# Alternating the closing steps of one attention half with the opening steps of the next, and running the down products one chunk later in place of two, in a four-layer cross-attention and feed-forward kernel

## The chip, the cores and the metric

The kernel is one program on one core of a Trainium2 chip. The metric is device time in microseconds (us) of one execution: 1136.41 us, the median of 3 runs. About 0.5% of it (5.7 us) is what a comparison can tell from no change.

## The reference

The input x has 4 batch rows ("streams") of 512 tokens by 128 features; the context has 77 tokens for each stream. Four layers follow one another, each an attention half and a feed-forward half, both added to x through a gate:

```
for l in 0..3:
    x = x + tanh(g_xattn[l]) * attention_l(layernorm(x), ctx)
    x = x + tanh(g_ffn[l])   * feed_forward_l(layernorm(x))
```

- attention 0, 1, 2: 16 heads of width 8, softmax over the 77 keys; attention 1 first works out a temperature for each head from statistics of the softmax; attention 2 has a padding mask. Attention 3 is one wide head with ReLU projections.
- feed-forward 0: 64 inner units with 16 hidden each; 1: a mixture of 4 experts of width 512, SiLU gated, top 2; 2: RMS norm and 8 experts of width 352, SiLU gated, top 2; 3: 8 linear experts, top 2.

All is float32; the expert products are made of three products of rounded parts.

## The kernel before, in words

The weights are loaded and turned once (the first 65 us). After that everything is in SBUF, and the only later transfers are the four stores of the result.

A *half* is one attention or one feed-forward of one layer and stream. Halves named ("A", i) for i = 0 to 11 are the multi-head attentions (kind A0 for i = 0 to 3, A1 for 4 to 7, A2 for 8 to 11); ("A", 12) to ("A", 19) are attention 3 and feed-forward 3 of the streams in turn (kinds A3, F3). ("F", 0) to ("F", 11) are the feed-forwards of layers 0 to 2 (kinds F0, F1, F2). So there are two tracks. Half ("F", i) runs beside ("A", i + 2), `beside` at line 727; ("F", 10) has 12 to 15 beside it and ("F", 11) has 16 and 17. I call such a pair of halves a stage.

Each engine (TensorE for matmuls, VectorE, ScalarE, GpSimd) has a queue of its own and works it off in order, with semaphores between engines. The order is fixed by hand: every half is a generator of *steps* on each engine, and all engines walk the same list `ORDER`. `turns` (line 729) makes it: `merged` (line 100) interleaves the steps of the attention half and of the feed-forward half of a stage in proportion to weights (`weights_a`, `weights_f`), so that both come to their ends together. A step's weight is thus the share of the other track that is laid beside it, not a time. A step that waits holds up all that stands behind it on its engine.

A multi-head half has three parts:

- `pre`, 28 steps (38 for A1). Step 0: VectorE takes the LayerNorm statistics (line 1034), GpSimd makes the inverse deviation (lines 804, 806); in kind A0 TensorE transposes the context (1372), which ScalarE copies in step 1. Step 2: K and V products on TensorE (1378, 1383), normalising on VectorE (1047), which waits for GpSimd. Step 3: ScalarE copies K and V out (868, 872), TensorE transposes the normalised x into bank `c` (1359). Step 4: ScalarE copies it to `xfa` (854), VectorE adds the rounding rest of K (1114). Step 5: VectorE lays the keys out by head (1128), and TensorE makes the first of four Q products (1392). Steps 9 to 24 (`S0` to `S1`) are 16 score blocks for the row maxima (1404, 1142), in A1 with exponentials and sums too.
- `body`, 17 steps: scores, exponential, product with V, and the turning of each group of four heads.
- `tail`, 7 steps, a chain across engines: ScalarE copies the last group out (`copy_out`, 846), TensorE turns it (`turn`, 1345), VectorE divides it (`divide`, 1018, 1020), TensorE transposes the whole (1665), ScalarE copies that (999), TensorE makes the product with Wo (1672, 1674), and VectorE adds it to x (1317).

`attention` (line 764) runs `pre`, `body` and `tail` of each half, and then those of the next. I call the steps from the last copy-out (846) of one half to the first Q product (1392) of the next a *seam*; there are eleven between the twelve multi-head halves.

The feed-forwards F1 and F2 go through 16 and 24 *chunks*, three steps each. TensorE makes the up product into a bank `UP` (three matmuls, lines 1585 to 1587), ScalarE takes a tanh of it into `hb` (983), VectorE multiplies (1286); TensorE makes the gate product into bank 5, VectorE multiplies by it (1277, signal `chunk_ready`). The gate product of the next chunk needs bank 5, and so waits for that signal. The `down` product (1597) takes `hb` and adds into bank 7; it is called `LATE` = 2 chunks later, and when an expert is whole VectorE adds it to x (`gated`, 1266). `hb` has three buffers: the tanh of chunk n waits for the down product of chunk n - 3.

Of the kernel before, what the change touches and what calls it, by code (L numbers as in the profile page):

```python
# [34 lines left out]
ACT = mybir.ActivationFunctionType  # L35
AX = mybir.AxisListType

P = 128
# [5 lines left out]
S2 = 77  # L44
S2E = S2 + S2 % 2
H = 16
HD = 8
G = 4
# [8 lines left out]
ATTENTIONS = 3 * STREAMS  # L57
# [5 lines left out]
F2 = 352  # L63
# [487 lines left out]
def main(nc, a, out, v):  # L551

    ctx, sb, sig, bank = v["ctx"], v["sb"], v["sig"], v["bank"]
# [3 lines left out]
    WqR, WkR, Wv, Wo, bo, ones_r, bcol, W3x, diag = (v[n] for n in (  # L557
        "WqR", "WkR", "Wv", "Wo", "bo", "ones_r", "bcol", "W3x", "diag"))
# [5 lines left out]
    KT, VP, lg, pk = (v[n] for n in ("KT", "VP", "lg", "pk"))  # L564

    m1_w1, m1_w3, m1_w2, m2_w1, m2_w2, m2_w3, m2_rms, m3_w, m3_b = (v[n] for n in (
        "m1_w1", "m1_w3", "m1_w2", "m2_w1", "m2_w2", "m2_w3", "m2_rms", "m3_w", "m3_b"))
# [12 lines left out]
    x, ctxn, mk, mr, x2p = (v[n] for n in ("x", "ctxn", "mk", "mr", "x2p"))  # L580
    in_x, in_ctx, masks_ready = (v[n] for n in ("in_x", "in_ctx", "masks_ready"))
    ctxT = each("ctxT", [P, S2])


    xfa = sb("xfa", [P, N])
    xff = two("xff", [P, N]) + [xfa]
    xna, xnf = sb("xna", [P, T, P]), sb("xnf", [P, T, P])
# [79 lines left out]
    NS = T * G  # L667
# [6 lines left out]
    S0 = Q0 + G  # L674
    S1 = S0 + NS
    RING = (1, 0, 2, 3)
    TURN = (4, 5)
    LATE = 2

    def ends_expert(k, n):  # L680
        return n + 1 == len(chunks[k]) or chunks[k][n + 1][0] > chunks[k][n][0]
# [13 lines left out]
    def steps_pre(k):  # L695
        if k in MHA:
            return S1 + (13 if k == "A1" else 3)
        return {"F0": 5, "A3": 12}.get(k, 11)

    def steps_body(k):  # L700
        if k in MHA:
            return H + 1
        return {"A3": 3, "F0": 2 * (C0 + 1), "F3": len(tiles)}.get(k) or 3 * (len(chunks[k]) + LATE)

    def steps_tail(k):
        return 7 if k in MHA else 2 if k == "F0" else 0

    def weights_a(u):

        k = kind(u)  # L710
        if k in MHA:
            block, after = (1.8, 0.8) if k == "A1" else (0.5, 0.6)
            return [1.0] * S0 + [block] * NS + [after] * (steps_pre(k) - S1) + [0.75] * steps_body(k) + [0.6] * steps_tail(k)
        return [1.0] * (steps_pre(k) + steps_body(k))

    def steps_f(u):
# [43 lines left out]
    UP = ups()  # L760

    def run(pre, body, tail):

        def attention():
            for i in range(ATTENTIONS + 2 * STREAMS):
                u = ("A", i)
                yield from chain(pre(u), body(u), tail(u))

        def feed_forward():
            yield from pre(("F", 0))  # L770
            for i in range(ATTENTIONS):
                u, n = ("F", i), steps_f(("F", i))
                last = i + 1 == ATTENTIONS
                m, ahead = (0, iter(())) if last else (steps_pre(kind(("F", i + 1))), pre(("F", i + 1)))
                sent = 0
                for at, _ in enumerate(chain(body(u), tail(u))):
                    while sent < m and (sent + 1) * n <= (at + 1) * m:
                        next(ahead)
                        sent += 1
                    yield  # L780
                assert sent == m and at + 1 == n and next(ahead, None) is None

        tracks = {"A": attention(), "F": feed_forward()}
        for half in ORDER:
            next(tracks[half])
        assert all(next(t, None) is None for t in tracks.values())

    with nc.Block() as block:
# [49 lines left out]
        def _(act):  # L838
# [9 lines left out]
            def pre(u):  # L848
                half, s, k, b = u[0], side(u), kind(u), stream(u)
                l = int(k[1])  # L850

                def normalized():
                    act.wait_ge(*x_turned.at(u, T - 1))
                    act.activation((xfa if half == "A" else xff[s])[:], bank[2 if half == "A" else UP[u, "x"]][:], ACT.Copy, scale=m2_rms[:, 0:1] if k == "F2" else 1.0) \  # L854
                        .then_inc(*xf_ready.up(u))

                for i in range(steps_pre(k)):
                    if k in MHA:
# [3 lines left out]
                        if i == 3:  # L862

                            if u[1]:
                                act.wait_ge(*keys_ready.at(("A", u[1] - 1), J - 1))
                            act.wait_ge(*k_psum.at(u))
                            for g in range(G):
                                act.activation(Ksp[:, g, :].bitcast(F32R), bank[0][0:QK, g * S2:(g + 1) * S2], ACT.Identity,
                                               bias=bcol[0:QK, l, 1, g:g + 1],
                                               accum_out=ksum[0:QK, g:g + 1] if l == 1 else None).then_inc(*k_high.up(u, g))  # L870
                            act.wait_ge(*v_psum.at(u))
                            act.activation(VP[:, :, 0:HD],
                                           bank[1][0:S2, 0:P].rearrange("p (h d) -> p h d", d=HD), ACT.Copy,
                                           scale=mk[b][:, 1:2] if l == 2 else 1.0).then_inc(*values_ready.up(u))
                        if i == 4:
                            normalized()
                        if Q0 < i <= Q0 + G:
# [449 lines left out]
        def _(pe):  # L1327
            reader = {}

            def free(b):  # L1330
                if b in reader:
                    signal, *key = reader[b]
                    pe.wait_ge(*signal.at(*key))
# [15 lines left out]
            def pre(u):  # L1349
                half, s, k, y = u[0], side(u), kind(u), stream(u)  # L1350
                l = int(k[1])

                c, xn, xf = (2, xna, xfa) if half == "A" else (UP[u, "x"], xnf, xff[s])

                def transpose_x():
                    free(c)
# [6 lines left out]
                for i in range(steps_pre(k)):  # L1363
# [4 lines left out]
                    if k in MHA:  # L1368
# [5 lines left out]
                        if i == 2:  # L1374
                            free(0)
                            pe.wait_ge(*ctx_ready.at(y))
                            for g in range(G):
                                op = pe.matmul(bank[0][0:QK, g * S2:(g + 1) * S2], WkR[l][:, g, :], ctxT[y][:], start=True, stop=True)
                            op.then_inc(*k_psum.up(u))
                            reader[0] = (k_low, u, G - 1)  # L1380

                            free(1)
                            pe.matmul(bank[1][0:S2, 0:P], ctxT[y][:], Wv[l][:], start=True, stop=True).then_inc(*v_psum.up(u))
                            reader[1] = (values_ready, u)
                        if i == 3:
                            transpose_x()
                        if Q0 <= i < S0:
                            g = i - Q0
                            b = RING[g % 4]
                            pe.wait_ge(*xf_ready.at(u))  # L1390
                            free(b)
                            pe.matmul(bank[b][0:QK, :], WqR[l][:, g, :], xf[:], start=True, stop=True).then_inc(*q_psum.up(u, g))  # L1392
                            reader[b] = (q_low, u, g)
                        if S0 <= i < S1:
                            n = i - S0
                            t, g = n // G, n % G
                            b = RING[(G + n) % 4]
# [75 lines left out]
                    elif k in router:  # L1473
                        w, b, E = router[k]
# [243 lines left out]
```

## Time and profile before

| what | us |
|---|---|
| median of 3 runs (1135.51 to 1141.63) | 1136.41 |
| the profiled execution, its own time | 1137.24 |
| its span, first to last instruction | 1135.5 |
| TensorE busy | 944.7 |
| VectorE busy | 711.9 |
| ScalarE busy | 459.6 |
| mean granted TensorE clock | 0.912 of full |

Busy time is the time in which an engine works on an instruction; a wait on a semaphore is not busy. A wait is put down to the instruction that ended it. In the profile, PE is TensorE, PEld its weight loads, DVE VectorE, ACT ScalarE and POOL GpSimd; L1317 is line 1317 of the kernel. A float32 product is two or more matmul instructions, so a line's count is larger than the number of products.

### The profile page before, as it was taken

The page shows a single profiled execution, that of the slowest core. Times are in us where ns is not written, and L with a number is a line of the kernel's source. Part 1 is how long each engine was busy: PE and PEld are TensorE (multiplying, and loading weights), DVE is VectorE, ACT ScalarE, POOL GpSimd, SP SyncE. Part 2 cuts the span into 40 slices and gives each one's busy share as a digit, 9 for nine tenths or more (in the row PEclk, how much of TensorE's full clock was granted, in tenths as well). Part 3 has the DMA queues.
Part 4 walks back from the last instruction along what each step waited for, and adds up shares of the span by engine and source line. Part 5 has one row for each costly group of instructions (what it writes and reads, how often), then busy time and mean ns, then how long its engine had stood idle before and what let it go on. Part 6 is the DMA issues. An engine that isn't in the chain of part 4 may idle for free.

```text
span 1135.5 us, 14471 instructions
## 1 busy us (share of the span) xinstructions
PE 944.7 (83%) x4795; PEld 624.7 (55%) x4795; DVE 711.9 (63%) x2190; ACT 459.6 (40%) x1101; POOL 105.9 (9%) x175
## 2 busy tenths in 40 slices
PE   2468899887777886987899899999999888979967
PEld 1434444433333355656567667666767666657744
DVE  0871433517538369579585665776776578887845
ACT  1515345455647645645635316335325222212110
POOL 3100000002103013012000100100100100000000
PEclk8669789999678898998999989999999899999987
DMA  9300000000000000000000000000000000000000
GB/s 262 118 1 1 1 1 1 1 1 1 0 1 1 1 1 1 1 1 1 1 1 2 1 1 1 1 1 1 1 1 1 1 1 10 1 10 1 1 10 9
DMA packets 12065, 12.72 MB, mean 11 GB/s; under 512 B 3758, under 2 KB 7896, under 8 KB 11992
## 3 DMA queue, kind: packets, MB, share of 16 engines
q10 hardware_dynamic: 5536, 8.04, 2.4%
q1 hardware_dynamic: 6072, 3.24, 1.1%
q0 software_dynamic: 384, 0.53, 0.3%
q8 instruction: 39, 0.64, 0.2%
q14 instruction: 34, 0.28, 0.1%
HBM read 10.75 MB, written 1.05 MB: 10 GB/s over the span
## 4 chain that ended last, share of the span: by engine, by line
PE 53%; DVE 28%; ACT 6%; issue 5%; POOL 2%; POOLq 0%; ACTq 0%; DVEq 0%
PE bank L1597 9%; PE bank L1585 5%; PE bank L1507 5%; PE bank L1587 4%; PE bank L1586 4%; PE bank L1392 4%; PE bank L1522 4%; DVE x L1302 3%; DVE hb L1286 3%; DVE nm L1142 3%; DVE hb L1277 3%; DVE x L1266 2%; PE bank L1562 2%; ACT PTs L946 2%; PE bank L1568 2%
## 5 line engine op out<-in xcount | busy, mean ns | idle before, releaser
L983 ACT ACTIVATE hb<-bank 96x512 f32<-96x512 f32 (+1 forms) x160 | 95.5, 597 | 262.6 <-PE bank L1587 261.7
L1585 PE MATMUL bank<-parts,m_w_lo 128*96 128x512 f32 (+1 forms) x320 | 151.0, 472 | 37.0 <-DVE hb L1277 30.0
L1597 PEld LDWEIGHTS bank<-m_w,hb 128*128 128x128 f32 (+1 forms) x1280 | 166.2, 197 | 26.8 <-issue 11.9
L1597 PE MATMUL bank<-m_w,hb 128*128 128x128 f32 (+1 forms) x1280 | 178.8, 284 | 0.5
L1286 DVE SCALAR_TENSOR_TENSOR hb<-hb,bank 96x512 f32<-96x512 f32 (+1 forms) x160 | 108.9, 680 | 87.8 <-ACT hb L983 87.4
L1587 PE MATMUL bank<-parts,m_w_hi 128*96 128x512 f32 (+1 forms) x320 | 128.9, 403 | 0.0
L1586 PE MATMUL bank<-parts,m_w_hi 128*96 128x512 f32 (+1 forms) x320 | 128.7, 402 | 0.0
L1277 DVE TENSOR_TENSOR hb<-hb,bank 96x512 f32<-96x512 f32 (+1 forms) x160 | 109.8, 686 | 11.5 <-PE bank L1587 6.4
L1585 PEld LDWEIGHTS bank<-parts,m_w_lo 128*96 128x96 f32 (+1 forms) x320 | 60.3, 189 | 82.6 <-DVE hb L1277 47.2
L1522 PE MATMUL bank<-Qs,KT 112*77 112x512 f32 x192 | 96.6, 520 | 6.8 <-ACT PTs L946 5.6
L1018 DVE RECIPROCAL rden<-bank 128x16 f32<-128x16 f32 x48 | 12.2, 255 | 130.8 <-PE bank L1345 130.8
L1142 DVE TENSOR_REDUCE nm<-bank 128x4 f32<-128x308 f32 x192 | 84.0, 471 | 15.6 <-PE bank L1412 10.4
L1404 PE MATMUL bank<-KT,Qs 96*128 96x308 f32 x192 | 77.0, 426 | 17.2 <-ACT PTs L892 12.5
L804 POOL TENSOR_SCALAR rstd_a<-mv_a 128x4 f32<-128x4 f32 x20 | 4.6, 228 | 830.5 <-DVE mv_a L1037 830.5
L1266 DVE SCALAR_TENSOR_TENSOR x<-bank,gw,x 128x128 f32<-128x128 f32 x192 | 53.9, 343 | 26.4 <-PE bank L1597 25.7
L1587 PEld LDWEIGHTS bank<-parts,m_w_hi 128*96 128x96 f32 (+1 forms) x320 | 59.9, 187 | 16.3
L1586 PEld LDWEIGHTS bank<-parts,m_w_hi 128*96 128x96 f32 (+1 forms) x320 | 60.4, 189 | 9.2 <-issue 3.4
L1404 PEld LDWEIGHTS bank<-KT,Qs 96*128 96x128 f32 x192 | 38.1, 202 | 42.2 <-ACT PTs L892 22.9
L1392 PE MATMUL bank<-xfa,WqR 128*96 128x512 f32 x96 | 54.2, 681 | 2.7 <-ACT xfa L854 2.7
L892 ACT ACTIVATE PTs<-bank,nms 128x77 f32<-128x77 f32 x128 | 39.9, 328 | 37.0 <-DVE nms L1161 37.0
L1507 PE MATMUL bank<-PTs,VP 77*32 77x512 f32 x384 | 54.5, 614 | 0.0
L846 ACT ACTIVATE Os<-bank 128x512 f32<-128x512 f32 x48 | 28.7, 598 | 61.0 <-PE bank L1507 61.0
(272 smaller groups left out, 1544.0 us busy)
## 6 DMA issues: line engine op xcount, KB each, us to landing
m_w<-in_L_ffn_w_dram ACTq DMA_DIRECT2D x2, 1024.0 KB, 11.4
nat_m<-in_L_ffn_W_dram ACTq DMA_DIRECT2D x1, 1408.0 KB, 16.7
x<-in_x_dram SPq DMA_DIRECT2D x4, 256.0 KB, 8.1
out_dram<-x SPq DMA_DIRECT2D x4, 256.0 KB, 2.0
f_out<-in_L_ffn_Wout_dram POOLq DMA_DIRECT2D x8, 64.0 KB, 7.9
m_w<-in_L_ffn_W_experts_dram ACTq DMA_DIRECT2D x1, 512.0 KB, 17.1
ctxn<-in_ctx_dram SPq DMA_DIRECT2D x4, 38.5 KB
Wq<-in_L_xattn_Wq_dram SPq DMA_DIRECT2D x2, 64.0 KB
```

The costliest lines, as they stand in the source:

```text
L983: act.activation(hb[n % 3][0:m, :], bank[UP[u, n]][0:m, :], ACT.Tanh, scale=0.5).then_inc(*chunk_act.up(u, n))
L1142: dve.tensor_reduce(nm[:, t, J * g:J * g + J], bank[RING[(G + n) % 4]][:, 0:J * S2].rearrange("p (h k) -> p h k", k=S2), AX.X, ALU.max, ne ...
L1277: dve.tensor_tensor(h, h, bank[TURN[1]][0:m, :], ALU.mult).then_inc(*chunk_ready.up(u, n))
L1286: dve.scalar_tensor_tensor(out=h, in0=h, scalar=1.0, in1=bank[UP[u, n]][0:m, :], op0=ALU.add, op1=ALU.mult) \
L1392: pe.matmul(bank[b][0:QK, :], WqR[l][:, g, :], xf[:], start=True, stop=True).then_inc(*q_psum.up(u, g))
L1404: op = pe.matmul(dst, Qs[0:QK, g, t * P:(t + 1) * P], KT[0:QK, J * g:J * g + J, :].rearrange("p h k -> p (h k)"), start=True, stop=l == 1)
L1507: op = pe.matmul(bank[2 + g % 2][32 * j:32 * j + 32, :], VP[:, h, :], PT[h % NPT][0:S2, :], start=True, stop=True, tile_position=(0, 32 * j))
L1522: pe.matmul(dst, KT[:, h, :], Qs[0:QK + H, h // J, :], start=l != 0, stop=True).then_inc(*scores_psum.up(u, h))
L1585: pe.matmul(dst, w_lo, x_hi, start=True, stop=False)
L1586: pe.matmul(dst, w_hi, x_hi, start=False, stop=False)
L1587: return pe.matmul(dst, w_hi, x_lo, start=False, stop=True)
L1597: op = pe.matmul(bank[7][:, t * P:(t + 1) * P], hb[n % 3][0:m, t * P:(t + 1) * P], wd, start=i == 0 and t == 0, stop=ends_expert(k, n) and ...
```

## The change

Three things are edited, and what they need.

1. In `attention`, the first `EARLY` = 6 steps of the next half's `pre` are issued between the seven steps of the tail, in turn: tail 0, pre 0, tail 1, pre 1, to tail 5, pre 5, tail 6. This is for the eleven seams between the halves 0 to 11; the tail of half 11, and everything after it, keep their order. The thirteen steps have a weight of 0.5 each; they had 0.6 for a step of the tail and 1.0 for each of the six. The six belong to the list of the earlier half now, so that they lie beside another feed-forward half than before.
2. So that both can be under way, banks are moved: the normalised x is turned into bank 1 (2 for A3 and F3), and V comes to stand beside K in bank 0, and is made and copied before K. The Q product into bank 0 waits for that copy as well.
3. `LATE` is 1 in place of 2: the down product of chunk n - 1 follows the gate product of chunk n, and a half of kind F1 or F2 has three steps fewer at its end.

```
-    LATE = 2
+    EARLY = 6
+    XA = {"A3": 2, "F3": 2}
+    LATE = 1
...
-            return [1.0] * S0 + [block] * NS + [after] * (steps_pre(k) - S1) + [0.75] * steps_body(k) + [0.6] * steps_tail(k)
+            pre = [1.0] * S0 + [block] * NS + [after] * (steps_pre(k) - S1)
+            tail = [0.6] * steps_tail(k) if u[1] + 1 == ATTENTIONS else [0.5] * (steps_tail(k) + EARLY)
+            return pre[EARLY if u[1] else 0:] + [0.75] * steps_body(k) + tail
...
         def attention():
+            ahead = pre(("A", 0))
             for i in range(ATTENTIONS + 2 * STREAMS):
-                u = ("A", i)
-                yield from chain(pre(u), body(u), tail(u))
+                yield from chain(ahead, body(("A", i)))
+                ahead = pre(("A", i + 1))
+                for at, _ in enumerate(tail(("A", i))):
+                    yield
+                    if i + 1 < ATTENTIONS and at < EARLY:
+                        next(ahead)
+                        yield
...
-                    act.activation((xfa if half == "A" else xff[s])[:], bank[2 if half == "A" else UP[u, "x"]][:], ACT.Copy, scale=m2_rms[:, 0:1] if k == "F2" else 1.0) \
+                    act.activation((xfa if half == "A" else xff[s])[:], bank[XA.get(k, 1) if half == "A" else UP[u, "x"]][:], ACT.Copy, scale=m2_rms[:, 0:1] if k == "F2" else 1.0) \
...
                             act.wait_ge(*k_psum.at(u))
+                            act.wait_ge(*v_psum.at(u))
+                            act.activation(VP[:, :, 0:HD],
+                                           bank[0][0:S2, G * S2:G * S2 + P].rearrange("p (h d) -> p h d", d=HD), ACT.Copy,
+                                           scale=mk[b][:, 1:2] if l == 2 else 1.0).then_inc(*values_ready.up(u))
...
-                            act.wait_ge(*v_psum.at(u))
-                            act.activation(VP[:, :, 0:HD],
-                                           bank[1][0:S2, 0:P].rearrange("p (h d) -> p h d", d=HD), ACT.Copy,
-                                           scale=mk[b][:, 1:2] if l == 2 else 1.0).then_inc(*values_ready.up(u))
...
-                c, xn, xf = (2, xna, xfa) if half == "A" else (UP[u, "x"], xnf, xff[s])
+                c, xn, xf = (XA.get(k, 1), xna, xfa) if half == "A" else (UP[u, "x"], xnf, xff[s])
...
                             pe.wait_ge(*ctx_ready.at(y))
+                            pe.matmul(bank[0][0:S2, G * S2:G * S2 + P], ctxT[y][:], Wv[l][:], start=True, stop=True) \
+                                .then_inc(*v_psum.up(u))
...
-                            free(1)
-                            pe.matmul(bank[1][0:S2, 0:P], ctxT[y][:], Wv[l][:], start=True, stop=True).then_inc(*v_psum.up(u))
-                            reader[1] = (values_ready, u)
...
                             free(b)
+                            if b == 0:
+                                pe.wait_ge(*values_ready.at(u))
```

## Rows read from the trace of the kernel before

**Rows 1.** The page: busy time by engine, and granted clock in 40 slices.
```profile
PE 944.7 (83%) x4795; PEld 624.7 (55%) x4795; DVE 711.9 (63%) x2190; ACT 459.6 (40%) x1101; POOL 105.9 (9%) x175
...
PEclk8669789999678898998999989999999899999987
```
**Rows 2.** Windows by stage: stretch, length, busy (count) of each engine, PEclk, DMA.
```profile
67.00:111.92 44.92, 38.51 (x189) 19.76 (x188) 15.56 (x43) 18.43 (x36) 1.28 (x2) 0.88 0.00 1
...
259.69:334.15 74.46, 54.63 (x174) 24.75 (x173) 37.17 (x115) 43.31 (x130) 13.50 (x20) 0.76 0.00 1
...
571.25:641.24 69.99, 67.78 (x388) 48.08 (x386) 47.29 (x134) 29.96 (x55) 2.52 (x4) 1.00 0.00 1
...
892.34:1135.50 243.16, 200.31 (x1085) 151.46 (x1083) 176.37 (x566) 46.57 (x86) 13.01 (x22) 0.93 0.01 5
```
**Rows 3.** Windows of the eleven seams: the first, the sum of the first six, the sum of all.
```profile
105.61:116.78 11.17, 6.48 (x33) 4.76 (x33) 5.67 (x29) 3.15 (x9) 2.51 (x4) 0.70 0.00 0
...
sum 70.97, PE 46.92 PEld 32.92 DVE 32.04 ACT 25.93 POOL 8.80; mean PE 7.82 PEld 5.49 DVE 5.34 ACT 4.32 POOL 1.47
...
sum 149.07, PE 111.55 PEld 84.92 DVE 84.23 ACT 52.35 POOL 21.74; mean PE 10.14 PEld 7.72 DVE 7.66 ACT 4.76 POOL 1.98
```
**Rows 4.** PE's waits from 105.6 to 892 us: total, times, longest.
```profile
PE bank L1585 <- DVE hb L1277: 18.7, 21, 2.1
...
PE bank L1665 <- DVE att L1020: 9.7, 12, 1.4
...
PE bank L1359 <- DVE xna L1047: 8.6, 7, 2.1
...
PE bank L1345 <- ACT Os L846: 4.7, 6, 0.8
PE bank L1672 <- ACT Os L999: 3.8, 6, 0.8
```
**Rows 5.** Timeline of the third seam, on PE.
```profile
208.49 1.16 PE L1674 MATMUL bank<-Wo,Os 128*128 128x128 f32 x8
...
213.45 1.01 PE L1359 MATMUL bank<-ident,xna 128*128 128x128 f32 x4 [1.95 <-DVE xna L1047]
...
215.16 1.09 PE L1392 MATMUL bank<-xfa,WqR 128*96 128x512 f32 x2
```
**Rows 6.** Timeline of the third seam, on DVE and ACT.
```profile
210.35 0.86 DVE L1034 BATCH_NORM_STATS2 stats_a<-x 128x6 f32<-128x128 f32 x4
...
212.96 1.11 DVE L1047 TENSOR_SCALAR xna<-x,mv_a,rstd_a 128x128 f32<-128x128 f32 x4 [1.46 <-POOL rstd_a L806]
214.11 0.92 DVE L1114 SCALAR_TENSOR_TENSOR Ksp<-bank,bcol,Ksp 32x77 f32<-32x77 f32 x4
...
215.14 1.24 DVE L1128 TENSOR_SCALAR KT<-Ksp,hmask 96x308 fp32r<-96x308 f32 x4
...
204.56 0.60 ACT L846 ACTIVATE Os<-bank 128x512 f32<-128x512 f32 x1 [1.73 <-PE bank L1507]
...
211.38 0.96 ACT L868 ACTIVATE Ksp<-bank,bcol 96x77 fp32r<-96x77 f32 x4
212.23 0.28 ACT L872 ACTIVATE VP<-bank 77x128 f32<-77x128 f32 x1
```
**Rows 7.** PE in the stretches of half clock that begin in seams or just behind.
```profile
110.10:120.40 10.30, 7.89 (x26) 0.50 0.00 0
...
sum 30.70, PE 26.59; mean PE 5.32
```
**Rows 8.** Timeline of the tenth seam, where the eighth feed-forward half begins.
```profile
719.16 0.50 PE L1585 MATMUL bank<-parts,m_w_lo 128*128 128x512 f32 x1 [2.13 <-DVE hb L1277]
...
716.02 0.74 DVE L1317 SCALAR_TENSOR_TENSOR x<-bank,gates_col,x 128x512 f32<-128x512 f32 x1
716.68 0.86 DVE L1034 BATCH_NORM_STATS2 stats_a<-x 128x6 f32<-128x128 f32 x4
...
718.42 0.69 DVE L1277 TENSOR_TENSOR hb<-hb,bank 128x512 f32<-128x512 f32 x1
```

## The prediction, made before the changed kernel was run

> **What bounds the kernel now.** I read the busy times of the page first, then the windows stage by stage, then the waits of PE, and last the timeline of single seams.
>
> PE is busy for 944.7 of 1135.5 us, DVE for 711.9, ACT for 459.6 [rows 1]. The reader is to see that no engine is full over the whole, but PE comes near, and that its clock is below full in the first half of the span and nearly full later. By stage there are three pictures [rows 2]. In the first ones (attention 0, alone or beside the light feed-forward 0) PE idles 44.92 - 38.51 = 6.4 us of 44.9. Where attention 1 lies beside feed-forward 0 nothing is full: PE 54.6, ACT 43.3 and DVE 37.2 of 74.5 us, at a mean clock of 0.76; here a chain across engines sets the time. With the expert halves PE is full: 67.8 of 70.0 us at full clock. In the last 243 us PE idles 43 us, but that stretch keeps its order, but for `LATE`.
>
> So where the first edit works, time is to be had only from PE's idle time and from its clock. The windows of the eleven seams give 149.07 us with PE busy for 111.55: 37.5 us idle, a quarter of the seams' length, against 2 us idle in a whole 70 us stage elsewhere [rows 2, 3]. PE's waits say what for [rows 4]: for the divided heads 9.7 us, the normalised x 8.6, the copy-outs 4.7 and 3.8. These are the links of two chains, the tail and the opening, run one after the other. (A few of the copy-out waits lie in a body, outside a seam.)
>
> **The change part by part.** *The alternation.* I take the third seam. It lasts from 204.56, where the copy-out starts, to the first Q product at 215.16: 10.6 us [rows 5, 6]. The tail's chain takes half of that, and the statistics of the next stream, which need nothing from it, start only at 210.35 [rows 6]. Now I lay the same instructions out in the new order, from the copy-out at 0, each in order on its engine. ACT: copy-out to 0.6. PE: turning the group 0.75 to 1.4. DVE: statistics 0 to 1.2, dividing from 1.4 to 1.95 (0.55 for its two instructions). POOL is done at 2.6, since 212.96 - 210.35 = 2.6 us pass from the start of the statistics to normalising, at which DVE now starts. PE: K and V from 1.4 to 2.6 (eight and two small matmul instructions; I allow 1.2 us), the divided heads to 3.2, x turned from 3.0 to 3.95. ACT: V and K together 1.24 us [rows 6], to 3.9, then the tail's copy to 4.5, and x to 5.1. PE: the product with Wo from 4.6 to 5.7 (1.16 us for its matmuls, [rows 5]), and the first Q product at 5.7. DVE: the rest of K and the keys (0.92 and 1.24 us, [rows 6]) end near 6.2, and the addition to x near 7.0.
>
> So a bare seam is 5.7 us long, of which PE works about 5, in place of 10.6. The feed-forward's share comes on top. By the weights of attention 0 the seam had (4.2 + 6) of 35.75, or 28.5% of the feed-forward beside it, and has 6.5 of 32.05, or 20%. That work goes nowhere else for free: it fills the blocks and the body, where PE is full in most stages. I count no gain for the move of it, only for the idle time. PE's waits by name in the seams and around them add up to 9.7 + 8.6 + 4.7 + 3.8 = 26.8 us [rows 4]. I take it that two thirds of them go, 18 us. The ends: nothing, if the alternated chains wait as long as the two did, and all 37.5 us of the seams [rows 3]. I choose near the middle, since my layout leaves some 0.7 us in a bare seam, and eleven of that are 8 us.
>
> *The clock.* Granted clock falls to half (1.2 of 2.4 GHz) just behind five of the seams. In the first seam PE was busy for 6.48 of 11.17 us, and from 110.1 the clock was half for 10.3 us, with PE busy for 7.89 of them. The five stretches make 30.7 us with PE busy for 26.59 [rows 3, 7]. At full clock their matmuls would need about half: 13.3 us is the upper end, and the lower is nothing, if the clock falls there all the same, or somewhere else. PE in the seams will be busy for some 80% in place of 75% on average, and in the first from 58% to near 85%. I take 6 us, a little under half of the upper end, because part of what a matmul takes in those stretches is already hidden behind ACT and DVE.
>
> [...] In this trace no single gap in the seams is longer than 2.1 us [rows 4], and the clock fell all the same. [...]
>
> *Work ahead of the chunks.* Where an expert half begins, its second gate product waits 2.13 us for DVE, which has the addition to x (0.74) and the statistics (0.86 and the aggregation after it) ahead of the chunk's two products [rows 8]. The statistics are a stage earlier now. Some four stages have this. Of 1.2 us each I take half, 2 us. The ends are nothing and 5 us.
>
> *What it costs.* No instruction is added, and no transfer is moved. K's copies stand behind V's, 0.28 us [rows 6], on the way to the keys; eleven of these are 3 us, and I count all of it as a loss, since block 0 waits for the keys. The extra wait ahead of the Q product into bank 0 is for this same copy, which is done three steps earlier: nothing. Moved to bank 1, the turned x has to wait for the last exponential of the body, which the last product with V has waited for already: nothing. The addition to x stands behind the keys now, and the fourth Q product needs bank 3 from it; it comes at 7.0 in my layout, and that Q product would start no earlier than 5.7 + 3 x 0.9 = 8.4. Nothing.
>
> *`LATE`.* The down product of chunk n - 1 needs `chunk_ready` of n - 1, and the gate product of chunk n, just ahead of it in PE's queue, has waited for that already, since both use bank 5. So the later call adds no wait. What waits for the down products is the tanh of three chunks on, which comes later still, and the addition of the whole expert, which keeps its distance to the next expert's first down product. Only the end of a half changes: one down product less behind the last gate product, and weights of 1.3 in place of 2.6 in some 42. PE does the same work; the last product by bank 5 on DVE (0.69, [rows 8]) is covered by the last down product but one, about 1 us of PE. If that cover is gone it costs some 0.7 us in each of 8 halves. I take nothing, with ends of -4 and +6 us.
>
> **The sum** is -18 - 6 - 2 + 3 = -23 us. Against the profiled execution's own 1137.24 us that is 1114.2; the median of the runs lies 0.8 us below that execution, so I forecast 1113.5 us.
>
> **The rivals.** *Only the light stages gain* (2 in 10). The first six seams, beside little or no expert work, have 24 of the 37.5 us idle (71.0 us long, busy for 46.9, [rows 3]). In the others PE has chunks to do in any case, and its idle time there is named after DVE's chunk products, 18.7 us in all [rows 4], which stay. If half of the light seams' idle time goes, and the clock gives nothing: 1124 us, in a range of 1122 to 1131.
>
> *The clock gives back more* (1 in 10). Everything behind the seams runs at full clock, and nearly all named waits go: -27 - 13 + 3 = -37 us, so 1099. For it speaks that attention 1's stages have a mean clock of 0.76 [rows 2], much of it lost outside the seams; against it, that their blocks are not edited.
>
> *The seams only change their place* (7 in 100). The merging is by proportion: less feed-forward in the seam means that PE may idle as long in a shorter seam, and the work moved to the blocks costs there what the seam saves. Then 1131 to 1142, no change that can be measured.
>
> *Slower* (8 in 100): DVE as the late one. In an alternated seam DVE's queue has statistics, division, normalising (behind POOL), K's rest (behind four copies on ACT), keys and the addition to x, nearly 6 us of work, on a stretch that is shorter, and a chunk's product that is queued behind any of them holds PE's next gate product. Rows 8 have the price of one such wait, 2.13 us. The seven seams with chunks beside them would need 12 more of them to eat up the 26 us of gains; with two in each seam, 14 of them or 30 us, the time is 1144. What speaks against it is that DVE is busy for 84 of 149 us in the seams [rows 3], and that the feed-forward steps between statistics and normalising are as many as before by weight.
>
> **How the numbers follow.** The likeliest case has 55 in 100, with a range of its own from 1104 to 1122 (half to one and a half of the sum's gain, cut where the neighbours begin). For 8 in 10 I reach down to 1098, which takes in the larger gain in the clock, and up to 1131, which takes in the light stages. Faster by over 0.5% (below 1130.7): 0.55 + 0.2 + 0.1 = 0.85. Within 0.5%: 0.07. Slower: 0.08.
>
> **What the profile after would show.** If the steps are right: (1) from the last copy-out to the first Q product some 7 to 8 us in the first four seams, in place of 10.6 to 11.8; (2) PE's waits for the divided heads and for the normalised x in those seams small, their sum from 18 to under 7 us; (3) no half-clock stretch behind the first and second seam; (4) the length of the stage with attention 2 beside the first expert halves nearly the same, within 3 us; (5) the last 243 us the same within 2 us; (6) PE's wait for DVE's chunk product (18.7 us before 892) no larger. The prediction fails if (6) grows by more than 10 us, if the clock falls as often at other places, or if ACT, which has the K and V copies ahead of the tail's copy, turns up as the one that PE waits for at the product with Wo.

## The result and the profile after

The changed kernel takes 1062.97 us (median of 4 runs, 1061.30 to 1065.34), against 1136.32 before (also 4 runs): a ratio of 0.9346, with a 95% interval of 0.9316 to 0.9377. It is faster by 73 us; I had forecast 23. The sign was right, and the size that I forecast was a third of what came.

The page after, for [rows 1] (lines of the kernel's text are 11 further on behind the edits, so L1585 is L1596 here, L1665 is L1676):
```profile
span 1063.6 us, 14472 instructions
PE 905.5 (85%) x4795; PEld 608.3 (57%) x4795; DVE 709.5 (67%) x2190; ACT 457.7 (43%) x1101; POOL 104.8 (10%) x175
...
PEclk9669999998898999999999999999999999999987
```
The span is 71.9 us shorter, and two numbers account for it. PE is busy for 39.2 us less (944.7 to 905.5) with the same 4795 instructions. And PE idles for 158.1 us in place of 190.8, which is 32.7 less. The busy times of the other engines moved by 2.4 us or less. That the shorter busy time is the clock can be checked: the clock was at half for 199.3 us of the span before and for 103.8 after, with PE busy for 148.7 and 76.6 us of them. At half clock a matmul takes about twice as long (the down product's 581 ns at the most, for a median of 275), so 72.1 us less of work at half clock should give back some 36 us; this is an estimate from these numbers, and 39.2 came. So the reader should look at both halves of "busy plus idle".

Windows by stage, for [rows 2]:
```profile
67.00:111.75 44.75, 39.63 (x201) 20.89 (x201) 19.87 (x63) 19.79 (x43) 2.09 (x3) 0.90 0.00 1
238.48:298.15 59.67, 46.98 (x173) 21.68 (x172) 36.14 (x114) 42.84 (x131) 13.43 (x20) 0.86 0.00 1
514.44:582.64 68.20, 67.21 (x383) 48.22 (x382) 47.37 (x135) 29.58 (x56) 2.51 (x4) 1.00 0.00 1
823.34:1063.60 240.26, 199.49 (x1101) 151.59 (x1099) 176.85 (x570) 47.46 (x87) 12.97 (x22) 0.95 0.01 5
```
Attention 1 beside feed-forward 0 went from 74.46 to 59.67 us, a stage of which neither the blocks nor the body were edited (only the share of the feed-forward half that lies beside them). The full stage, attention 2 beside an expert half, lost 1.8 us and the end 2.9.

The eleven seams, for [rows 3]: the first, the third, the seventh, the sum of the first six and the sum of all.
```profile
105.20:110.70 5.50, 4.26 (x33) 3.54 (x34) 3.90 (x20) 2.81 (x9) 1.26 (x2) 1.00 0.00 0
...
186.20:192.60 6.40, 5.29 (x39) 4.20 (x40) 3.55 (x14) 3.98 (x11) 0.79 (x1) 1.00 0.00 0
...
428.70:435.70 7.00, 7.00 (x53) 6.09 (x54) 5.42 (x23) 3.64 (x13) 1.26 (x2) 1.00 0.00 0
...
sum 35.80, PE 27.37 PEld 22.94 DVE 23.28 ACT 20.81 POOL 6.51; mean PE 4.56 PEld 3.82 DVE 3.88 ACT 3.47 POOL 1.09
...
sum 85.60, PE 76.78 PEld 65.57 DVE 66.24 ACT 42.47 POOL 12.81; mean PE 6.98 PEld 5.96 DVE 6.02 ACT 3.86 POOL 1.16
```
They are 85.6 us long in place of 149.1, and PE idles in them for 8.8 in place of 37.5.

PE's waits from 105 to 818 us, for [rows 4]:
```profile
PE bank L1596 <- DVE hb L1288: 10.8, 11, 1.9
...
PE bank L1683 <- ACT Os L1010: 4.6, 6, 0.9
PE bank L1356 <- ACT Os L857: 4.1, 6, 0.8
```
The waits for the divided heads (9.7 before) and for the normalised x (8.6) are gone from this list. The two for a copy of ACT in the tail stay (3.8 and 4.7 us before, 4.6 and 4.1 now), and so does what the chunks wait for, at 10.8 for 18.7.

The third seam, for [rows 5] and [rows 6], shows the order that I had laid out by hand: PE, then DVE, then ACT.
```profile
186.98 0.63 PE L1356 MATMUL bank<-ident,Os 128*128 128x128 f32 x4 [0.59 <-ACT Os L857]
...
189.19 0.60 PE L1676 MATMUL bank<-ident,att 128*128 128x128 f32 x4
...
189.63 0.60 PE L1370 MATMUL bank<-ident,xna 128*128 128x128 f32 x4
...
191.58 1.16 PE L1685 MATMUL bank<-Wo,Os 128*128 128x128 f32 x8
...
187.65 0.26 DVE L1029 RECIPROCAL rden<-bank 128x16 f32<-128x16 f32 x1 [2.09 <-PE bank L1356]
...
188.15 1.11 DVE L1058 TENSOR_SCALAR xna<-x,mv_a,rstd_a 128x128 f32<-128x128 f32 x4
...
189.61 0.95 ACT L883 ACTIVATE Ksp<-bank,bcol 96x77 fp32r<-96x77 f32 x4
...
190.44 0.60 ACT L1010 ACTIVATE Os<-bank 128x512 f32<-128x512 f32 x1
```
From the copy-out at 186.24, the divided heads are turned 2.95 us later, x 3.4, the product with Wo starts at 5.3 and the first Q product at 6.3. In my layout the last two were at 4.6 and 5.7; the rest agrees within half a microsecond. (This seam has steps of feed-forward 0 in it, such as L1573 and L1667, which are left out above; my layout was for a bare one.)

### The profile page after: what moved, and what is told of

Same layout as the page of the kernel before. It is cut to its first block, busy times and chain, and to the rows that moved or that the text cites. A ratio compares the mean times of both kernels' runs of the same rounds, so it can differ in the third digit from the quotient of the medians.

```text
span 1063.6 us, 14472 instructions
## 1 busy us (share of the span) xinstructions
PE 905.5 (85%) x4795; PEld 608.3 (57%) x4795; DVE 709.5 (67%) x2190; ACT 457.7 (43%) x1101; POOL 104.8 (10%) x175
## 4 chain that ended last, share of the span: by engine, by line
PE 57%; DVE 23%; ACT 6%; issue 5%; POOL 2%; POOLq 0%; ACTq 0%; DVEq 0%
PE bank L1608 10%; PE bank L1596 6%; PE bank L1518 5%; PE bank L1598 5%; PE bank L1597 5%; PE bank L1533 4%; PE bank L1403 4%; DVE x L1313 3%; DVE nm L1153 3%; DVE hb L1297 3%; DVE hb L1288 2%; ACT PTs L957 2%; PE bank L1573 2%; DVE x L1277 2%; PE bank L1356 2%
## 5 line engine op out<-in xcount | busy, mean ns | idle before, releaser
L1596 PE MATMUL bank<-parts,m_w_lo 128*96 128x512 f32 (+1 forms) x320 | 151.9, 475 | 29.9 <-DVE hb L1288 20.5
L1608 PE MATMUL bank<-m_w,hb 128*128 128x128 f32 (+1 forms) x1280 | 175.4, 281 | 2.2 <-DVE hb L1288 2.0
L1598 PE MATMUL bank<-parts,m_w_hi 128*96 128x512 f32 (+1 forms) x320 | 127.2, 398 | 0.0
L1597 PE MATMUL bank<-parts,m_w_hi 128*96 128x512 f32 (+1 forms) x320 | 127.0, 397 | 0.0
L1596 PEld LDWEIGHTS bank<-parts,m_w_lo 128*96 128x96 f32 (+1 forms) x320 | 59.0, 184 | 78.1 <-DVE hb L1288 32.6
L1598 PEld LDWEIGHTS bank<-parts,m_w_hi 128*96 128x96 f32 (+1 forms) x320 | 58.8, 184 | 16.1
L1597 PEld LDWEIGHTS bank<-parts,m_w_hi 128*96 128x96 f32 (+1 forms) x320 | 59.2, 185 | 9.5 <-issue 4.5
L1277 DVE SCALAR_TENSOR_TENSOR x<-bank,gw,x 128x128 f32<-128x128 f32 x192 | 53.9, 343 | 11.0 <-PE bank L1608 10.8
L1415 PEld LDWEIGHTS bank<-KT,Qs 96*128 96x128 f32 x192 | 37.1, 194 | 35.0 <-ACT PTs L903 15.4
L857 ACT ACTIVATE Os<-bank 128x512 f32<-128x512 f32 x48 | 28.7, 597 | 54.2 <-PE bank L1518 54.2
L1533 PEld LDWEIGHTS bank<-Qs,KT 112*77 112x77 f32 x192 | 28.9, 152 | 39.8 <-ACT PTs L957 25.9
L834 POOL TENSOR_TENSOR PTs<-PTs 128x308 f32<-128x308 f32 x64 | 44.2, 700 | 71.6 <-ACT PTs L903 53.8
```

The costliest lines, as they stand in the source:

```text
L1277: op = dve.scalar_tensor_tensor(out=x[b][:, t, :], in0=bank[7][:, t * P:(t + 1) * P], scalar=gw[s][:, t, e:e + 1], in1=x[b][:, t, :], op0= ...
L1415: op = pe.matmul(dst, Qs[0:QK, g, t * P:(t + 1) * P], KT[0:QK, J * g:J * g + J, :].rearrange("p h k -> p (h k)"), start=True, stop=l == 1)
L1533: pe.matmul(dst, KT[:, h, :], Qs[0:QK + H, h // J, :], start=l != 0, stop=True).then_inc(*scores_psum.up(u, h))
L1596: pe.matmul(dst, w_lo, x_hi, start=True, stop=False)
L1597: pe.matmul(dst, w_hi, x_hi, start=False, stop=False)
L1598: return pe.matmul(dst, w_hi, x_lo, start=False, stop=True)
```

## The experiments

Each is a kernel of its own, timed against the kernel before on the same chip. The table has the median, the ratio with its interval, and from the profile of one of its executions PE's busy and idle time and the mean granted clock. "Dummies" are added matmuls on constants, whose result nobody reads. The mean clock takes in the part ahead of the first seam as well, where the order is nearly the same in all: half clock there lasted from 37.5 to 47.8 us while that part stayed 103 to 106 us long. So 0.005 of a mean clock, and some 2 us of a single profile's length, say nothing on an edit.

| kernel | median us | ratio [95%] | PE busy | PE idle | clock |
|---|---|---|---|---|---|
| before | 1136 to 1140 | 1 | 944.7 | 190.8 | 0.912 |
| changed | 1063.0 | 0.9346 [0.9316, 0.9377] | 905.5 | 158.1 | 0.951 |
| LATE back at 2 | 1075.0 | 0.9447 [0.9425, 0.9470] | 912.9 | 159.8 | 0.933 |
| LATE = 1 alone | 1127.7 | 0.9907 [0.9872, 0.9943] | 942.4 | 179.2 | 0.912 |
| in series | 1127.9 | 0.9911 [0.9876, 0.9945] | 940.6 | 188.1 | 0.918 |
| weight 0.785 (its profile: an execution of 1101) | 1087.6 | 0.9545 [0.9494, 0.9595] | 931.7 | 167.6 | 0.924 |
| weight 0.6 | 1075.3 | 0.9438 [0.9396, 0.9480] | 912.6 | 159.3 | 0.936 |
| weight 0.35 | 1074.9 | 0.9442 [0.9418, 0.9465] | 919.9 | 155.0 | 0.933 |
| alternation alone | 1092.0 | 0.9599 [0.9569, 0.9629] | 922.7 | 165.0 | 0.934 |
| first six seams | 1081.6 | 0.9505 [0.9464, 0.9546] | 915.2 | 165.4 | 0.938 |
| EARLY = 3 (its trace: a second run) | 1073.9 | 0.9420 [0.9372, 0.9469] | 916.6 | 156.7 | 0.933 |
| dummies in before | 1129.2 | 0.9916 [0.9887, 0.9946] | 955.2 | 174.1 | 0.919 |
| twice the dummies | 1132.2 | 0.9907 [0.9869, 0.9945] | 964.8 | 166.7 | 0.922 |
| dummies in changed | 1070.2 | 0.9397 [0.9375, 0.9420] | 922.0 | 145.2 | 0.944 |

**Which part gains: LATE.**
```
# of the changed kernel
-    LATE = 1
+    LATE = 2
```


> The changed kernel with LATE back at 2 (and so two drain chunks at the end of an expert half). PE's busy time fell by 39 us with the change (944.7 to 905.5) and its idle time by 33 (190.8 to 158.1). If alternating the seams did all of it, and LATE nothing, as predicted: 1060 to 1069 us. If the down product one chunk earlier helps by its own: over 1070 us, with the loss in the stages with expert halves (405 us and later in the kernel before).

```
# of the kernel before
-    LATE = 2
+    LATE = 1
```


> The kernel before with LATE = 1 alone. If LATE is neutral: 1133 to 1140 us. If it gives something by itself: under 1130 us.

Neither is neutral: 12 us by the one (the ratios are a percentage point apart, and the intervals do not touch), 10 by the other. So LATE has a share that I had put at nothing. But it does not show in one place. Alone it took 11.6 us of PE's idle time and 2.3 of its busy time (in an execution of 1123.3 us, 4 under the median). In the changed kernel the idle times are 1.7 us apart, and the rest is busy time. Windows from the tail of half 3 to that of half 7, first with LATE at 2, then the changed kernel:
```profile
233.80:517.90 284.10, 231.85 (x1085) 144.74 (x1086) 200.52 (x616) 181.82 (x540) 54.36 (x80) 0.89 0.00 1
```
```profile
234.70:510.10 275.40, 223.21 (x1088) 136.70 (x1089) 200.06 (x616) 179.97 (x539) 54.26 (x80) 0.94 0.00 1
```
8.7 of the 9.1 us between the two spans arise in this stretch, and 8.6 of them are PE's busy time, at a clock of 0.89 against 0.94. It can be placed more closely. From the last copy-out of half 3 to that of half 5 only feed-forward 0 lies beside, which has no chunks, so the order is the same in both kernels, and so are length and clock (121.8 and 122.6 us, 0.87 both). In the next two halves, beside experts, it is 162.4 us at 0.89 with LATE at 2 and 153.0 at 0.99 with 1.

What LATE shortens can be seen in part: VectorE waited 25.7 us in the kernel before for a down product, ahead of adding an expert to x, and 13.0 with LATE = 1 alone; PE's waits for VectorE's chunk product went from 30.0 to 23.2. In return PE now waits for that product ahead of the down product too, 6.5 us in place of 1.7 (weight loads and matmuls counted together). That these waits are the 10 us is not shown.

**Which part gains: the alternation or the weights.**
```
# of the changed kernel: same steps, weights and banks
                for _ in tail(("A", i)):
                    yield
                for _ in range(EARLY if i + 1 < ATTENTIONS else 0):
                    next(ahead)
                    yield
```


> The changed kernel, with its banks, its weights, its LATE and its stage limits, but the seven tail steps issued first and the six opening steps behind them. Theory one (the alternation itself shortens the seams, and the clock follows): the time goes back to 1120 to 1140 us, with the seams 10 us long again. Rival (it is the new weights, which move feed-forward work out of the seams to places where it fills gaps, that gain): under 1100 us, though the seams stay long.

1127.9 us, the time of LATE alone. The new weights, the new stage limits and the moved banks give nothing that can be measured while the two chains run one after the other; the seams are 136.0 us long again with PE busy for 95.7:
```profile
sum 136.00, PE 95.69 PEld 75.58 DVE 73.44 ACT 44.51 POOL 13.84; mean PE 8.70 PEld 6.87 DVE 6.68 ACT 4.05 POOL 1.26
```
All else equal the alternation is worth 65 us, 30 of it idle time and 35 busy time, and 50 of it lie in the seams (136.0 to 85.6).

```
# of the changed kernel (0.785, then 0.6, then 0.35)
-... [0.5] * (steps_tail(k) + EARLY)
+... [0.785] * (steps_tail(k) + EARLY)
```


> The changed kernel with a weight of 0.785 for each of the thirteen steps, so that a seam has the share of the feed-forward half that it had before (10.2 in all). Alternation as the cause: 1060 to 1075 us, since PE is filled either way. If the moved feed-forward work is what gained: 1085 us or more.

> The changed kernel with a weight of 0.6 for the thirteen steps (0.5 gave 1063 us, 0.785 gave 1088, 0.35 gave 1075). Theory: the order sets how often the clock falls in the stages of halves 5 to 8, so the time need not be smooth in the weight, but TensorE's idle time is: 1065 to 1085 us, idle 158 to 166 us, and most of the difference to the changed kernel in TensorE's busy time. Rival, idle time decides: idle grows by as much as the time does.

> The changed kernel with a weight of 0.35 in place of 0.5 for the thirteen steps, so still less feed-forward in a seam. If the gain of the weight (25 us between 0.785 and 0.5) is of work that moves to where TensorE has gaps, it goes on: 1050 to 1060 us. If 0.5 is near the point where a seam has just enough to fill it: 1060 to 1075 us, with TensorE waiting in the seams again.

1087.6, 1075.3 and 1074.9 us, with 1063.0 at 0.5. Idle time goes one way with the weight: 155.0, 158.1 and 159.3 us from 0.35 to 0.6. Busy time does not: 919.9, 905.5, 912.6. So in these profiles a larger share of the feed-forward in a seam costs a little idle time, and what sets 0.5 apart from its two neighbours is busy time. At 0.35 that lies in the stages of halves 4 to 7, which are 15.4 us longer than at 0.5, with 71.7 us at half clock in place of 34.1. The mean clock of a whole execution is no safe guide to it: one at 0.35 had 0.942 and took 1073.95 us, one of the changed kernel 0.945 and 1062.80.

The idle and busy time of the 0.785 kernel in the table (167.6 and 931.7) come from an execution of 1101 us, at the lowest clock of its four, where its fastest took 1082.67; they are no measure of the weight. The next run gives one, by comparison with LATE back at 2.

```
# both: LATE = 2 and a weight of 0.785
```


> The kernel before with the alternation alone: LATE = 2, and 0.785 for each of the thirteen steps, so that a seam has its old share of the feed-forward half. If the three parts add up (73 us in all, some 25 for the weight and 10 for LATE): 1095 to 1103 us. If they need each other: 1105 us or more.

1092.0 us: the alternation gives some 46 us with the seam's old share of the feed-forward, somewhat more than the 35 to 43 us that my expectation left for it. From here the changed kernel can be reached by two ways. The weight first gives 17 us and LATE then 12; LATE first gives 6 and the weight then 23 (from the ratios, times 1138). The 6 and the 23 rest on the ratio at 0.785, whose interval (0.9494 to 0.9595) overlaps that of this run, so it is not shown that the weight and LATE help each other. The 17 us are clear: 9.8 of busy time and 5.2 of idle time in the two profiles (922.7 to 912.9, 165.0 to 159.8).

**Where it gains.**
```
# of the changed kernel: alternate for i < 6; behind it, for the later seams,
+                for _ in range(EARLY if 6 <= i < ATTENTIONS - 1 else 0):
+                    next(ahead)
+                    yield
```


> The changed kernel with the steps alternated in the first six seams alone; in the last five the tail comes first and the six opening steps behind it, with the same weights. If only the light stages gain by the alternation: 1060 to 1068 us. If the seams with expert work gain as well, by the 8 us of idle time that the change took out of them and by the clock in the stages of halves 7 to 9: 1075 to 1095 us.

1081.6 us: the five seams with experts beside them are worth 18 us (0.9505 to 0.9346), so they gain as well. From the last copy-out of half 7 to that of half 11 this run is 9.4 us longer than the changed kernel, 8.1 of it idle time. The rest lies one stage earlier. The stage whose opening seam is the first in series again, from tail to tail, here and in the changed kernel:
```profile
430.60:515.00 84.40, 71.01 (x372) 50.42 (x371) 62.52 (x185) 46.64 (x139) 13.70 (x20) 0.92 0.00 1
```
```profile
433.10:510.10 77.00, 65.44 (x373) 47.24 (x372) 62.28 (x184) 46.17 (x137) 13.66 (x20) 0.98 0.00 1
```
It is 7.4 us longer, 5.6 of it busy time. In the three stages ahead of it, from the last copy-out of half 3 to that of half 6, the order is the same in both, and there they agree: 199.3 and 198.5 us at a clock of 0.91 and 0.92. So in this stage the clock, 0.92 in place of 0.98, went with the stage's own order.

```
# of the changed kernel
-    EARLY = 6
+    EARLY = 3
```


> The changed kernel with EARLY = 3: statistics, normalising and the K and V products alternate with the tail, and the x transposes, the copies and the first Q product follow behind it. A seam should last about 8 us in the first four, between 5.5 and 10.6. If seam length decides: 1085 to 1105 us. If the start of statistics and GpSimd's part (2.6 us) was the main of it: under 1080 us.

> The kernel with EARLY = 3 once more, for a trace: the profiled execution of its first run took 4677 us, and the other three 1069 to 1077 us. If that was no property of the kernel: 1068 to 1078 us. Seams of 7 to 9 us in the first four, and TensorE's idle time 3 to 10 us above the changed kernel's 158.

1073.9 us in the first, and one execution of 1075.0 with a usable trace. The first six seams last 6.3, 6.3, 7.1, 6.4, 9.0 and 7.9 us, where I had expected 7 to 9 in the first four. Statistics, GpSimd and the K and V products are the main of it: with these three steps comes 5.8% of the 6.5%, of which LATE and the new weights in series have 0.9. (The run changes one thing more: the other three opening steps keep their weight of 1.0 and stay in the next half's list.) My expectation of 3 to 10 us more idle time was wrong; it has 156.7 us, and the difference is busy time again.

**Does filling TensorE's gaps hold the clock?**
```
# of the kernel before, in the first six seams
+            def fill(b, times):
+                for _ in range(times):
+                    pe.matmul(bank[b][:, 0:T * S2], identb[:], mask_q[:]..., start=True, stop=True)
...
+                        if i == 0:
+                            fill(0, 2)
+                        if i == 3:
+                            free(3)
+                            fill(3, 6)
+                        if i == Q0:
+                            fill(3, 3)
...
+                    if k in MHA and u[1] < 6 and i in (1, 3, 5):
+                        fill(1, 3)
```


> The kernel before with matmuls on constants that nobody reads added to TensorE's queue in the first six seams, where it waits (three ahead of the turning, of the divided heads and of the product with Wo, two with the first opening step, six ahead of the turned x, three ahead of the first Q product). The chain through the seam is as long as before, only TensorE's gaps are filled. If the clock is what the seams' idle time cost in the stages behind them: no half-clock stretch behind the first three seams, and 1112 to 1127 us. If the gain came from the shorter chain alone: 1134 to 1142 us.

The same with 4, 14, 6 and 6 in place of 2, 6, 3 and 3:

> The kernel before with twice as many unread matmuls in the first six seams (six ahead of each link of the tail, four with the first opening step, fourteen ahead of the turned x, six ahead of the first Q product), so that TensorE's gaps there are full even at full clock. Three such matmuls in each place took the half-clock time from 153 to 136 us and the median from 1139.5 to 1129. If gaps in the seams are what lets the clock fall in the stages of halves 4 to 7 too: half-clock time under 110 us, and 1115 us or less in spite of some 10 us of added work. If the falls inside those stages have their cause there: half-clock time stays at 125 us or more, and the time is 1130 to 1142.

1129.2 and 1132.2 us, both with a ratio of 0.99: some 1% by filling alone, with both chains still in series. It is less than the clock theory wanted, and more than none. Half-clock time behind the first 80 us was 127.7 us in the stronger one, for 151.5 in the kernel before, and its time is 1132 us: of the two cases that I had set out for it, the one for causes inside the later stages held. The stronger one, from the first tail to the fourth and from there to the eighth:
```profile
108.00:252.80 144.80, 135.69 (x708) 71.51 (x707) 57.81 (x187) 68.61 (x129) 7.55 (x12) 1.00 0.00 1
252.80:564.30 311.50, 258.80 (x1210) 158.61 (x1209) 201.78 (x616) 180.64 (x541) 54.67 (x80) 0.87 0.00 1
```
and the kernel before and the changed one over the same halves:
```profile
108.40:256.60 148.20, 129.09 (x583) 64.89 (x584) 57.85 (x187) 68.83 (x130) 7.55 (x12) 0.92 0.00 1
...
256.60:568.10 311.50, 246.38 (x1096) 148.72 (x1094) 201.70 (x616) 180.59 (x541) 54.66 (x80) 0.87 0.00 1
```
```profile
108.50:234.70 126.20, 117.69 (x584) 60.36 (x583) 56.90 (x187) 68.04 (x132) 7.55 (x12) 1.00 0.00 1
```
In the three stages of attention 0 full gaps bring the clock from 0.92 to 1.00, worth 3.4 us of length after what the added matmuls cost; the changed kernel has that clock too and is 18.6 us shorter still. No gap that was filled was longer than 2.1 us. (The Trainium skill, page "TensorE: Matmul & The Clock Gate", section "A second HAM failure mode: psum-queue depth-cycling", tells of a kernel in which short idle times between groups of matmuls made the clock go to and fro between its two levels. The 0.92 and 1.00 here agree with it.) In the four stages of attention 1, of which three have a filled seam, they bring nothing: 311.5 us and 0.87, as before. The changed kernel has 0.94 there, and 275.4 us.

```
# of the changed kernel, halves 4 and 5, into bank 6 while nobody reads it
+                            fill(u, 3)      # ahead of each score block
...
+                        fill(u, 2)          # ahead of each score product
```


> The changed kernel with such matmuls ahead of each score block (three) and each score product (two) of halves 4 and 5, attention 1 beside feed-forward 0, where 31 us are at half clock and TensorE idles for 28. If those stages are slow by the clock: half clock gone there, 1050 to 1058 us. If they are bound by ScalarE and VectorE, and the clock only follows: 1062 to 1070 us with the half clock gone as well.

1070.2 us, 7 slower, and neither theory's picture. Those two stages took 126.8 us in place of 121.8, at a mean clock of 0.89 for 0.87:
```profile
233.10:359.90 126.80, 108.88 (x487) 54.22 (x487) 75.94 (x252) 87.80 (x265) 27.01 (x40) 0.89 0.00 1
```
The added work took 9 us of idle time in them and hardly moved the clock, so this run says nothing on what a full clock there would give.

## Why the prediction was wrong, point by point

*What bounds it.* Right: time came from PE's idle time and from its clock, and the full stage that I had shown lost 1.8 us.

*The seams.* The layout was right: 5.7 us for a bare seam, and the first two last 5.5 and 5.7. The sum over them was too small. I took two thirds of the named waits, 18 us; idle time fell by 32.7, of which 28.7 in the seams (37.5 to 8.8). The waits for the divided heads and the normalised x went nearly whole, while the two behind ACT's copies stayed. And there was idle time in the seams beyond the waits that I had named, above all beside the experts: in the last five seams it went from 13.5 to 0.4 us. The far end of my range, all 37.5 us of the seams, was closer than the middle that I chose.

*The clock* is the step that failed: "The five stretches make 30.7 us [...] At full clock their matmuls would need about half: 13.3 us is the upper end". I chose 6 us; it gave back 39.2. I had counted the half-clock stretches behind a seam alone, and called the blocks and bodies of attention 1 unedited, so that their mean clock of 0.76 [rows 2] was no part of any term (only of a rival). It was the larger part. From the tail of half 3 to that of half 7 alone PE's busy time fell by 23.2 us (246.4 to 223.2), with the clock from 0.87 to 0.94. In the three stages of attention 0, where my term applied, it fell by 11.4 (129.1 to 117.7), inside the end that I had given. The upper end was no bound at all, since it was drawn around the stretches next to the edit; the run with six seams shows a whole stage's clock fall from 0.98 to 0.92 when its opening seam is put back in series.

*The share of the feed-forward in a seam*: "I count no gain for the move of it, only for the idle time." That is a second term put at nothing, and it was worth 17 us (1092.0 to 1075.0, both with LATE at 2). It is so only with the alternation: in series the new weights gave nothing that can be measured.

*LATE* at nothing, with ends of -4 and +6: wrong by 10 to 12 us. The argument that the down product waits for nothing new is not quite so: PE's waits for VectorE ahead of it went from 1.7 to 6.5 us with LATE = 1 alone. What the earlier call gives back is more than that, once mostly in idle time and once in clock; by which link stays open.

*The costs* (3 us for V ahead of K) show nowhere; no wait of PE for the keys is among its longest. *Work ahead of the chunks* was in the right direction and too small: 2 us forecast, and the wait went from 18.7 to 10.8.

*The signs to look for.* Held: waits, no half clock behind the first two seams (clock 1.00 from 108 to 235 us), the full stage within 3 us, no more waiting for chunks. The first four seams last 5.5 to 6.6 us, below the 7 to 8 that I gave. ACT's copy ahead of the product with Wo, which I had named as a sign of failure, is one of two links of the tail that PE still waits for: 4.6 us, for 3.8 before. Not held: the last stretch within 2 us; it gained 2.9. Only LATE is edited there, and it is LATE's gain: from the last copy-out of half 11 to the end it is 254.5 us before, 254.3 with LATE back at 2, 251.0 in the changed kernel and in the run in series.

*The rivals.* "Only the light stages gain" is refuted by the run with six seams. "The clock gives back more" was the right direction, at 1 in 10 and with an end at 1099. Its condition, that all behind the seams runs at full clock, did not come true (0.94 in halves 4 to 7). "Slower" and "the seams only change their place" have nothing left: the seams lost 28.7 us of idle time and the whole span 32.7, so none of it came back elsewhere.

What stays open is how the order of a stage sets its clock. Filled gaps in the seams do so in attention 0's stages and not in attention 1's; the alternation, its weight, EARLY and LATE each moved the clock there by some hundredths, LATE in both directions (from half 3 to half 7 its half-clock time went from 81.9 to 99.0 us by LATE alone, and from 64.9 to 34.1 beside the alternation). PE's longest waits there, four for a product of VectorE (L1167, now L1178), are as long after as before (9.1 and 10.4 us in all), so they are not what the change took away. I have runs for the size of it (half-clock time and the busy time in it) and none for the cause.

## What to carry to other kernels

Where two chains of short links across engines follow one another and the second does not need the first, issue them in turn: the eleven seams went from 149.1 to 85.6 us here, and in-order queues did not turn that into new waits. Price a change in TensorE's idle time in two terms, the idle time and the busy time at half clock, and take the upper end of the second from every half-clock stretch of the stages touched, not from those beside the edit alone. And time neighbours of a schedule's weights: 0.35 and 0.6 were both 12 us behind 0.5 by their medians, and in their profiles nearly all of it was busy time.

## What the hardware showed that I had not expected

The same program with the same inputs took from 1082.67 us (mean clock 0.941; another had 1082.71 at 0.933) to 1092.49 us (0.928) at weight 0.785, while the changed kernel's four runs, at 0.945 to 0.951, lie within 4 us. Whether the order decides how far the time scatters is not shown by four runs of each.

One execution took 4677 us, that of EARLY = 3 under its first profile. Its page:
```profile
PE 4619.3 (99%) x4795; PEld 2815.6 (60%) x4795; DVE 729.1 (16%) x2190; ACT 471.4 (10%) x1101; POOL 104.6 (2%) x175
...
L1608 PE MATMUL bank<-m_w,hb 128*128 128x128 f32 (+1 forms) x1280 | 911.0, 1050 | 0.0
```
A down product's matmul has a mean of 1050 ns for 281 in the changed kernel, PE alone is slow (VectorE's 729.1 us are near its 709.5), and the granted clock is noted as 1.0. What slowed it is open. It did not come back in the other four executions of the same kernel (1069 to 1077 us).
